# Matching the work of two engines: GpSimd makes a third of two integer products, VectorE takes a maximum one block late

## The reference, cut to what matters

```python
def act_qdq(x):
    qmax = 2.0 ** (ACT_BITS - 1) - 1.0          # ACT_BITS = 16
    scale = jnp.maximum(jnp.max(jnp.abs(x)) / qmax, 1e-12)
    return jnp.clip(jnp.round(x / scale), -qmax - 1.0, qmax) * scale
x = act_qdq(x)
up = act_qdq(x @ lpbq_dequant(w_up).T)
gate = act_qdq(x @ lpbq_dequant(w_gate).T)
sig = fixed_qdq_u16(jax.nn.sigmoid(gate))
gate = act_qdq(gate * sig)
o = act_qdq(gate * up)
return o @ lpbq_dequant(w_down).T
```

## Time and profile before

| | us |
|---|---|
| median of three runs | 1425.21 (1425.14 to 1425.28) |
| the profiled execution's own time | 1423.45 |
| its span, first to last instruction | 1421.7 |
| VectorE busy over the span | 1056.5 (74%) |
| ScalarE busy | 973.9 (69%) |
| GpSimd busy | 346.7 (24%) |
| TensorE busy | 1259.1 (89%) |

### The profile page before, as it was taken

The page is one execution under the profiler, slowest core; times in us unless marked ns, Lnnn a source line. Parts: engine busy times, 40 slices in busy tenths (PEclk is TensorE's granted clock), DMA queues, the critical chain, the costliest instruction groups (busy, mean ns, idle before and its releaser), DMA issues. The chain is left out here.

```text
span 1421.7 us, 25336 instructions
## 1 busy us (share of the span) xinstructions
PE 1259.1 (89%) x8412; PEld 671.9 (47%) x8412; DVE 1056.5 (74%) x2561; ACT 973.9 (69%) x1690; POOL 346.7 (24%) x555
## 2 busy tenths in 40 slices
PE   7787999999999999999999999999997699930397
PEld 4333344344334334334434434436886588720397
DVE  4366788888887887888888888872564466999687
ACT  4434777777777777777777777773675558969672
POOL 4544121211211211212112112004462002420033
PEclk9989999999999999999999999999998899975599
DMA  8999987878878788798698796625321222837033
GB/s 245 306 337 257 249 225 225 227 208 243 221 219 234 219 232 221 204 259 212 200 260 219 207 249 190 199 71 180 105 75 45 104 89 84 287 107 261 0 95 114
DMA packets 263759, 273.14 MB, mean 192 GB/s; under 512 B 66222, under 2 KB 246990, under 8 KB 259534
## 3 DMA queue, kind: packets, MB, share of 16 engines
q1 hardware_dynamic: 261998, 268.39, 65.0%
q10 hardware_dynamic: 1632, 3.15, 0.7%
HBM read 153.69 MB, written 117.00 MB: 190 GB/s over the span
## 5 line engine op out<-in xcount | busy, mean ns | idle before, releaser
L604 ACT ACTIVATE pr<-scoresT 128x512 f32<-128x512 f32 x1024 | 548.1, 601 | 210.0 <-PE scoresT L856 151.7
L851 PE MATMUL scoresT<-qT,kT 99*128 99x512 bf16 (+7 forms) x1408 | 355.5, 326 | 5.2 <-DVE attn_out L741 2.3
L701 DVE TENSOR_REDUCE mx<-scores_for_max 128x1 f32<-128x888 f32 (+6 forms) x448 | 301.6, 673 | 0.0
L696 DVE CUSTOM_DVE_ANT_0 junk<-scores_for_max,win 128x200 f32<-128x200 f32 (+2 forms) x512 | 179.9, 351 | 157.4 <-PE scores_for_max L823 147.8
L699 DVE TENSOR_REDUCE mx<-scores_for_max 128x1 f32<-128x64 f32 (+6 forms) x448 | 277.4, 619 | 0.0
L869 PE MATMUL attn_out<-pr,vS 128*17 128x512 f32 x2048 | 270.3, 600 | 6.0 <-DMA vS<-v_all 5.9
L851 PEld LDWEIGHTS scoresT<-qT,kT 99*128 99x128 bf16 (+1 forms) x1408 | 107.3, 97 | 333.7 <-ACT rows L581 97.0
L856 PE MATMUL scoresT<-idf,win 128*128 128x128 f32 (+1 forms) x1024 | 200.4, 256 | 0.0
L478 POOL COPY rows<-rows 128x736 f32<-128x736 f32 x128 | 102.2, 798 | 378.6 <-ACT rows L581 378.6
L822 PE MATMUL scores_for_max<-kX,qT 64*128 64x512 bf16 x512 | 167.3, 384 | 4.0 <-DVE mx L701 3.0
L823 PE MATMUL scores_for_max<-kX,qX 64*128 64x512 bf16 x512 | 167.3, 384 | 0.0
(11 more groups left out here) (218 smaller groups left out, 1979.3 us busy)
## 6 DMA issues: line engine op xcount, KB each, us to landing
rel_table<-rows SPq DMA_DIRECT2D x128, 512.0 KB, 4.8
win<-rel_table SPq DMA_DIRECT2D x128, 512.0 KB, 5.4
up_raw<-xT_normed SPq DMA_DIRECT2D x6, 1536.0 KB, 9.4
xT_normed<-up_raw SPq DMA_DIRECT2D x6, 1536.0 KB, 6.5
qT<-q_parts SPq DMA_DIRECT2D x32, 256.0 KB, 7.7
kX<-k_parts SPq DMA_DIRECT2D x64, 128.0 KB, 5.0
kT<-k_parts SPq DMA_DIRECT2D x32, 256.0 KB, 5.7
q_parts<-shared SPq DMA_DIRECT2D x32, 192.0 KB, 4.4
```

What stands on the lines that cost most here:

```text
L604: nc.scalar.activation(pr[:, n % NPR, h, :], bank, ACT.Exp).then_inc(t_read, 1)
L696: last = nc.vector.tensor_tensor_reduce(junk[:, n % 2, 0:z - a], bank[:, a:z], win[:, T % NW, q4, h, u:u + z - a], 1.0, NEG, ALU.add, ALU. ...
L701: last = nc.vector.tensor_reduce(mx[:, T % 2, q4, h, 2:3], bank[:, z:L], AX.X, ALU.max)
L851: last = mm(bank[:, a:e], k[0:r], q[0:r, a:e], start=(n == 0), stop=not near and n == len(pieces) - 1, skip_group_check=True)
```

## The change

In blocks 1 to 6 (`SHARED`) VectorE multiplies only the first 2048 columns (`REST`) in both stages. The last 1024 columns (`THIRDS[2]`) are made by GpSimd in `product_third`: it copies both 16-bit integer operands to float32 (`factor`, which takes the place of the residual buffers `res`), waits for its own copies, and multiplies them into `raw`. VectorE's maximum of such a block waits for it (`p_g2`, `p_o`). ScalarE, before it overwrites a buffer of integers, also waits until GpSimd has read it (`p_pg`, `p_po`). GpSimd does its third of block n right behind its rounding of sigmoid n; in the second stage its thirds stand between the reductions for scales 3 and 4. In the second stage VectorE takes the maximum of block k - 1 behind the multiply of block k (`largest_product`). SyncE issues the first two residual loads behind the reloads of the up blocks, when GpSimd's last product is done, as their buffers hold the factors until then.

```diff
@@ -1601,6 +1601,8 @@
     ORDER = KEPT + [j for j in range(NBLK) if j not in KEPT]
     THIRDS = [slice(t * 2 * HALF, (t + 1) * 2 * HALF) for t in range(3)]
     WHOLE = [slice(0, FT * HALF)]
+    SHARED = range(1, NBLK - 1)
+    REST = slice(0, 4 * HALF)
 
     def pieces(k):
 
@@ -1609,6 +1611,14 @@
     def handed(k, t):
 
         return t + 1 if k == 0 else k + len(THIRDS)
+
+    def own(k):
+
+        return [REST] if k in SHARED else pieces(k)
+
+    def thirds_till(k):
+
+        return sum(j <= k for j in SHARED)
 
     ctx = ExitStack()
     with ctx:
@@ -1637,6 +1647,9 @@
         wdh = wgh[:].rearrange("p c n -> p (c n)")
         wdl = wgl[:].rearrange("p c n -> p (c n)")
         res = [old_int[:, (4 + 2 * j) * 2 * HALF:(6 + 2 * j) * 2 * HALF].bitcast(F32).rearrange("p (q d) -> p q d", d=D) for j in range(2)]
+
+
+        factor = [old_int[:, (4 + 2 * j) * 2 * HALF:(6 + 2 * j) * 2 * HALF].bitcast(F32) for j in range(2)]
 
         f_xi = sem("f_xi")
         f_xh = sem("f_xh")
@@ -1650,11 +1663,15 @@
         f_sig = sem("f_sig")
         f_si = sem("f_si")
         f_g2 = sem("f_g2")
+        p_g2 = sem("p_g2")
+        p_pg = sem("p_pg")
         f_g2max = sem("f_g2max")
         f_umax = sem("f_umax")
         f_g2i = sem("f_g2i")
         f_ui = sem("f_ui")
         f_o = sem("f_o")
+        p_o = sem("p_o")
+        p_po = sem("p_po")
         f_omax = sem("f_omax")
         f_link = sem("f_link")
         u_st = [sem(f"u_st{j}") for j in range(2)]
@@ -1701,12 +1718,13 @@
                     load_parts(j + 3)
                 sp.wait_ge(f_out, M_ALL + FT * (j + 1))
                 sp.dma_start(ud[j], ub[j % 2]).then_inc(u_st[j % 2], 16)
-            for n in range(2):
-                sp.dma_start(res[n], rows_of(h2d, n)).then_inc(o_ld[n], 16)
             for j in range(NBLK - 2):
                 sp.wait_ge(u_st[j % 2], 16 * (j // 2 + 1))
                 sp.wait_ge(f_ui, j + 1)
                 sp.dma_start(ub[j % 2], ud[j]).then_inc(u_ld[j % 2], 16)
+            sp.wait_ge(p_o, len(SHARED))
+            for n in range(2):
+                sp.dma_start(res[n], rows_of(h2d, n)).then_inc(o_ld[n], 16)
             for n in range(2, NBLK + 2):
                 if n < NBLK + 1:
                     sp.wait_ge(o_fin, n - 1)
@@ -1731,6 +1749,15 @@
                 pool.wait_ge(wd_high, j + 1)
                 nc.gpsimd.tensor_tensor(wdl[:, c], plain, wdh[:, c].bitcast(F32), ALU.subtract).then_inc(wd_low, 1)
 
+            def product_third(read, done, k, to, one, other):
+
+                if k - 1 in SHARED:
+                    pool.wait_ge(done, thirds_till(k - 1))
+                nc.gpsimd.tensor_copy(factor[0], one[:, THIRDS[2]]).then_inc(read, 1)
+                nc.gpsimd.tensor_copy(factor[1], other[:, THIRDS[2]]).then_inc(read, 1)
+                pool.wait_ge(read, 2 * thirds_till(k))
+                nc.gpsimd.tensor_tensor(to, factor[0], factor[1], ALU.mult).then_inc(done, 1)
+
             scale_pool(pool, 1)
             pool.wait_ge(f_xg, NBLK)
             for n in range(NBLK):
@@ -1739,10 +1766,17 @@
                 for t, c in enumerate(pieces(n)):
                     pool.wait_ge(f_sig, handed(n, t))
                     nc.gpsimd.tensor_scalar(sig[n % 2][:, c], raw[:, n, c], U16, 1.0, ALU.mult, ALU.mult).then_inc(f_si, 1)
+                if n in SHARED:
+                    pool.wait_ge(f_si, handed(n, 2))
+                    product_third(p_pg, p_g2, n, raw[:, n, THIRDS[2]], gi[n % 2], sig[n % 2])
                 if 2 <= n < 5:
                     split_down(n - 2)
             scale_pool(pool, 2)
             scale_pool(pool, 3)
+            for k in SHARED:
+                pool.wait_ge(f_ui, k + 1)
+                pool.wait_ge(f_g2i, handed(k, 2))
+                product_third(p_po, p_o, k, raw[:, UP[ORDER[k]], THIRDS[2]], gi[k % 2], ui[k % 2])
             scale_pool(pool, 4)
             for n in range(NBLK + 1):
                 norm_rstd(pool, 2 * NBLK + n, n % 2 if n < NBLK else 2, wait)
@@ -1762,6 +1796,8 @@
             def round_gate(n):
                 if n >= 2:
                     act.wait_ge(f_g2, handed(n - 2, 2))
+                if n - 2 in SHARED:
+                    act.wait_ge(p_pg, 2 * thirds_till(n - 2))
                 for c in pieces(n):
                     nc.scalar.activation(gi[n % 2][:, c], raw[:, n, c], ACT.Identity, scale=inv[:, 1:2]).then_inc(f_gi, 1)
 
@@ -1781,6 +1817,8 @@
                 j = ORDER[k]
                 if k >= 2:
                     act.wait_ge(f_o, handed(k - 2, 2))
+                if k - 2 in SHARED:
+                    act.wait_ge(p_po, 2 * thirds_till(k - 2))
                 if j not in KEPT:
                     act.wait_ge(u_ld[j % 2], 16 * (j // 2 + 1))
                 nc.scalar.activation(ui[k % 2], ub[j % 2], ACT.Identity, scale=inv[:, 2:3]).then_inc(f_ui, 1)
@@ -1874,7 +1914,7 @@
             dve.wait_ge(t_inv, 2)
             nc.vector.tensor_scalar(coarse[:, 0:1], step[:, 1:2], 1.0 / U16, None, ALU.mult).then_inc(f_link, 1)
             for n in range(NBLK):
-                for t, c in enumerate(pieces(n)):
+                for t, c in enumerate(own(n)):
                     dve.wait_ge(f_si, handed(n, t))
                     nc.vector.tensor_tensor(raw[:, n, c], gi[n % 2][:, c], sig[n % 2][:, c], ALU.mult).then_inc(f_g2, 1)
                 largest_up(n)
@@ -1882,6 +1922,8 @@
                     dve.wait_ge(f_umax, NBLK)
                     largest_of(dve, 2)
                 dve.wait_ge(f_g2, handed(n, 2))
+                if n in SHARED:
+                    dve.wait_ge(p_g2, thirds_till(n))
                 if n < NBLK - 1:
                     largest(3, n, raw[:, n, :], f_g2max)
             largest(3, NBLK - 1, raw[:, NBLK - 1, 0:4 * HALF], f_g2max)
@@ -1892,14 +1934,23 @@
             scale_of(dve, 3, f_link, 3, coarse[:, 0:1])
             dve.wait_ge(t_inv, 4)
             nc.vector.tensor_tensor(coarse[:, 1:2], step[:, 2:3], step[:, 3:4], ALU.mult).then_inc(f_link, 1)
+
+            def largest_product(k):
+                n = UP[ORDER[k]]
+                dve.wait_ge(f_o, handed(k, 2))
+                if k in SHARED:
+                    dve.wait_ge(p_o, thirds_till(k))
+                largest(4, n, raw[:, n, :], f_omax)
+
             for k in range(NBLK):
                 n = UP[ORDER[k]]
                 dve.wait_ge(f_ui, k + 1)
-                for t, c in enumerate(pieces(k)):
+                for t, c in enumerate(own(k)):
                     dve.wait_ge(f_g2i, handed(k, t))
                     nc.vector.tensor_tensor(raw[:, n, c], gi[k % 2][:, c], ui[k % 2][:, c], ALU.mult).then_inc(f_o, 1)
-                dve.wait_ge(f_o, handed(k, 2))
-                largest(4, n, raw[:, n, :], f_omax)
+                if k:
+                    largest_product(k - 1)
+            largest_product(NBLK - 1)
             dve.wait_ge(f_omax, NBLK)
             largest_of(dve, 4)
             scale_of(dve, 4, f_link, 7, coarse[:, 1:2])
```

## The result

The changed kernel takes 1437.09 us (median of four runs, 1434.91 to 1439.21) against 1425.24 (1425.14 to 1425.44), slower by 11.85 us. The recorded ratio with its 95% interval is 1.0092 [1.0072, 1.0112], some 10 to 16 us; it is not simply that of the two medians, which is 1.0083. The forecast was 1429.8, slower by 4.6. Its direction held, and so did its first cause; the size did not.

A forecast was written before the change was run, and what follows sets the result against it. VectorE alone was taken to bound both stages, with GpSimd becoming the bound after the change. +2.3 us per stage, other edits nothing, made +4.6 on the profiled 1423.45, or 1429.8 against the median; range 1422 to 1438.

The forecast's parts named there:

- GpSimd becomes the bound by exclusion: First stage: GpSimd and VectorE exclude each other, so GpSimd's blocks take 9.3 or 11.25 us in series; +2.3 us.
- Unit costs: Per block: GpSimd's 1024-column copy 1.04 us and float multiply 2.36, VectorE's 2048-column multiply 2.28.
- slow copies: Rival: GpSimd's copies from integers take 1.2 us or more; 1433.6 at 1.2, 1438.4 at 1.4; chance 0.15.
- Second stage without the load: Second stage: six blocks of 6.5 us take 39.0 instead of 39.93, plus 3.27 for a second maximum at the end; +2.3.
- The use given for the late maximum: Second stage: a multiply needn't stand behind a maximum that waits for GpSimd; counted within the 6.5 us a block.
- The code load: Between scales 3 and 4: loading GpSimd's ordinary code back, at most 7.2 us, is hidden before block 1; costs nothing.
- a code load becomes visible: Rival: a code load or residual load is exposed; up to +5.7 us more, 1435.5; chance 0.03.
- The load for scale 4 and the residual loads: End of second stage: scale 4's 5.7 us load hides under 9.9 of VectorE's work, residual loads have 15 to spare; nothing.
- Thirds beside VectorE: Rival, both stages: GpSimd's copies and multiply run under VectorE's multiply without exclusion; 1416.4 us; chance of faster 0.12.

The follow-up runs named there:

- e2: GpSimd's thirds in the first product stage alone, second stage as in the kernel before; 1428.29 us, ratio 1.0032.
- e1: Changed kernel plus a one-column GpSimd addition right behind the reduction for scale 3, to load the ordinary code early; 1431.39 us, ratio 1.0051.
- e6: Changed kernel with the early code load and each second-stage maximum right behind its own multiply; 1431.35 us, ratio 1.0051.
- e5: Kernel before with only the second stage's maximum of the product taken one block late; 1427.11 us, ratio 1.0015.
- e4: Changed kernel with early code load, GpSimd's two copies and multiply replaced by four fills, last third of shared products left zero; 1418.5 us, ratio 0.996.
- e9: Changed kernel, late code load, with second and later reloads of up blocks held back until GpSimd's first second-stage product; 1440.53 us, single run.
- e3: GpSimd's thirds and the late maximum in the second stage alone, first stage as in the kernel before; 1434.08 us, ratio 1.0068.
- e13: Changed kernel with GpSimd's share cut to 512 columns in both stages, early code load and prompt maximum, run a second time; 1423.67 us, ratio 1.0002.

## Why the prediction was half right

**GpSimd becomes the bound by exclusion: right.** First stage +2.3 forecast, +2.40 in after and +2.69 in e2. The forecast had GpSimd start on block 7 at 1264.5; it started at 1265.60 in an execution that ran 1.0 late.

**Unit costs: right.** Copy 1.04 taken and measured, from unsigned integers too; product 2.36 and 2.35; VectorE's 2048 columns 2.28 and 2.29. The slow copies fell.

**Second stage without the load: right in the sum, in part by luck.** +2.3 forecast, +2.07 in e1, with blocks of 6.46 for 6.5 and one more maximum at the end (+3.2). But from block 1's multiply to block 7's took 37.80 in e1 (1292.13 to 1329.93) and not 39.0, since block 2's comes 5.49 behind block 1's; and the last multiply, forecast unchanged, is held by GpSimd's last third:

```profile
1329.93 4.33 DVE L1952 TENSOR_TENSOR raw<-xT_normed,shared 128x3072 f32<-128x3072 int16 x1
```

The first is 1.2 less than forecast, the second 0.9 more. The use given for the late maximum, that a multiply needn't stand behind a maximum that waits, is not in the 6.5: e6 has 6.46 without it. e5 measures the late maximum alone, in the kernel before, at +2.2 in the stretch.

**The code load: wrong, and in the stretch it is the whole miss.** The step was "The load back, at most from 1187.0 to 1194.2 = 7.2, stands before block 1, over 9 us after scale 3: nothing." The size was about right (8.43 and 8.79 measured, 1.2 and 1.6 over that bound). The place was not: a term put at nothing cost 6.5. I took the load to follow the reduction, since in before it starts right behind one, under line 1741. But there the next instruction in the queue, a rounding, is what calls for it, even while it waits for ScalarE. In after two copies stand first, which don't call for it and wait for ScalarE; so the load starts only when they are done, with nothing above it. e1 moves it and gives back 6.5 in the stretch, 5.0 by the medians. The case was in the rivals as "a code load becomes visible", priced at up to 5.7 by the reductions' load and given a chance of 0.03: its price should have been the 7.2 of the same load in the other direction.

**The load for scale 4 and the residual loads: right.** The reductions' configuration for scale 4 is issued at 1335.5 and GpSimd then waits for VectorE until 1345.32; the residual loads go out at 1335.3, land in 3.9 to 4.9 and nobody waits.

**Thirds beside VectorE: fell**, and e4 shows what it would have taken, work on GpSimd that reads nothing from the buffers.

**The sum.** 2.4 + 2.1 + 6.5 = 11.0, against 10.93 in the stretch; with the 1.0 it began late this is 11.9, less 0.5 behind it, and the profiled executions differ by 1434.91 - 1423.45 = 11.46.

**The range.** 1437.09 lies inside 1422 to 1438, but by luck: that end was set by slow copies up to 1.4, which fell, and the case that did come, a visible load, had been priced to 1435.5 only.

## What to carry to other kernels

When GpSimd alternates between code libraries, look for the first instruction that needs the new one, not for the switch: put a trivial instruction of that kind right behind the last use of the old code, so that the load runs in idle time. Before giving GpSimd a part of VectorE's two-input work, count both engines' reading instructions in series; what VectorE is spared is then the most that can be won, and only if GpSimd has room left in that sum. Work that fills a gap and is moved one step later leaves the gap empty and turns up at the end, as in e5.

## What the runs showed of the hardware

- GpSimd's copies from 16-bit integers to float ran behind a reduction over partitions without a code load (after, 1289.90 and 1293.01); the two-input addition of e1 (load at 1282.2) and the multiply of after (1294.1) needed one, and so did a rounding in before (1187.0). The load started only when that instruction was next in the queue.
- The load back left a gap of 7.33 with no traffic (e9), 6.97 in e1, where the DMA engines were 0.56 busy, and 6.75 to 7.30 in the other runs with an early load. It was 8.43 (after) and 8.79 (e3) with the DMA engines 0.82 to 0.84 busy; the load for a reduction left 5.8.
- GpSimd's fills (0.95 for 1024 columns) didn't hold a VectorE multiply (2.27) nor wait for it in e4; its copies (3.16 instead of 1.04), casts (3.34 instead of 0.61) and products (4.33 instead of 2.36) waited, and where they came first the multiply did (3.54 instead of 2.81 in e13).
